# Three reorderings in a two-layer attention and feed-forward kernel: an affine step one fill earlier, a vector step behind the next one, and a weight update behind a small norm

## What is computed

```
x = x + xattn0(ctx, layernorm(x))   # 8 heads of 128; keys and values from [layernorm(ctx)*g+b ; layernorm(x)*g'+b']
x = x + ffn0(layernorm(x))          # GELU(h) with W1 and W2 each plus a small update made from rows of the same batch
x = x + xattn1(layernorm(x), ctx)   # one head of 256
x = x + experts(layernorm(x))       # 8 gated experts, weighted
```

## Time and profile before

| What | Value |
|---|---|
| median of 3 runs (lowest to highest) | 1850.38 us (1848.1 to 1851.29) |
| profiled execution, its own time | 1849.33 us |
| its span in the trace | 1847.5 us, so 1.83 us lie around the span |
| TensorE busy | 1796.0 us, 97% of the span |
| VectorE, ScalarE, GpSimd busy | 79%, 72%, 29% |
| granted TensorE clock, mean | 0.996 of full speed |
| TensorE in the chain of waits that ended last | 80% of the span |

### The profile page before, as it was taken

The page is one execution under the profiler, slowest core; times in us unless marked ns, Lnnn a source line. Parts: engine busy times, 40 slices in busy tenths (PEclk is TensorE's granted clock), DMA queues, the critical chain, the costliest instruction groups (busy, mean ns, idle before and its releaser), DMA issues.

```text
span 1847.5 us, 40072 instructions
## 1 busy us (share of the span) xinstructions
PE 1796.0 (97%) x12874; PEld 1668.1 (90%) x12874; DVE 1464.4 (79%) x3530; ACT 1328.2 (72%) x2554; POOL 535.6 (29%) x700
## 2 busy tenths in 40 slices
PE   7999999999999999999899999999999999999999
PEld 5888888888888888888788999999999999999998
DVE  6888788887888777887667888888888888888876
ACT  4787777877778777777766777677667767766753
POOL 2444334543354433544533111011111111111100
PEclk9999999999999999999999999999999999999999
DMA  4454555645554434444627543333434333343300
GB/s 143 101 137 105 140 131 130 147 97 139 141 129 87 96 79 95 98 85 92 126 67 259 157 89 73 79 66 76 88 59 87 83 68 72 70 87 74 72 7 13
DMA packets 355420, 182.25 MB, mean 99 GB/s; under 512 B 292512, under 2 KB 340512, under 8 KB 355360
## 3 DMA queue, kind: packets, MB, share of 16 engines
q1 hardware_dynamic: 346656, 146.88, 32.9%
q0 software_dynamic: 8704, 34.61, 10.4%
HBM read 97.29 MB, written 21.23 MB: 64 GB/s over the span
## 4 chain that ended last, share of the span: by engine, by line
PE 80%; DVE 9%; issue 4%; ACT 3%; DMA 2%; POOL 1%; SPq 0%; DVEq 0%; POOLq 0%; ACTq 0%
PE ring L2049 9%; PE ring L2051 9%; PE ring L2050 8%; PE ring L741 8%; PE ring L743 8%; PE ring L742 8%; PE sim L2051 3%; PE sim L2049 3%; PE sim L2050 3%; PE sim L741 2%; PE sim L743 2%; PE sim L742 2%; DVE a_parts L664 2%; PE ps_x L741 2%; DVE a_nmax L644 2%
## 5 line engine op out<-in xcount | busy, mean ns | idle before, releaser
L410 POOL TENSOR_SCALAR a_parts<-a_pr,a_rinv 128x512 f16<-128x512 f32 x240 | 173.3, 733 | 489.0 <-DVE a_rinv L655 435.5
L2049 PE MATMUL ring<-b_xch,b_wel 128*128 128x256 f32 x1024 | 289.7, 283 | 0.5 <-DVE b_act_e L1672 0.5
L2051 PE MATMUL ring<-b_xcl,b_weh 128*128 128x256 f32 x1024 | 286.4, 280 | 0.0
L2050 PE MATMUL ring<-b_xch,b_weh 128*128 128x256 f32 x1024 | 286.0, 279 | 0.0
L503 ACT ACTIVATE a_pr<-sim,a_nmax 128x512 f32<-128x512 f32 x256 | 173.1, 683 | 44.2 <-DVE a_nmax L644 43.8
L2050 PEld LDWEIGHTS ring<-b_xch,b_weh 128*128 128x128 f32 x1024 | 193.4, 189 | 0.0
L2049 PEld LDWEIGHTS ring<-b_xch,b_wel 128*128 128x128 f32 x1024 | 192.1, 188 | 0.7 <-DVE b_act_e L1672 0.7
L2051 PEld LDWEIGHTS ring<-b_xcl,b_weh 128*128 128x128 f32 x1024 | 192.1, 188 | 0.0
L644 DVE TENSOR_REDUCE a_nmax<-sim 128x1 f32<-128x512 f32 x256 | 165.0, 681 | 30.3 <-PE sim L743 30.3
L1385 ACT ACTIVATE b_heh<-b_act_e 128x512 fp32r<-128x512 f32 x128 | 80.7, 630 | 146.9 <-DVE b_act_e L1672 113.0
L664 DVE SCALAR_TENSOR_TENSOR a_parts<-a_pr,a_rinv,a_parts 128x512 f16<-128x512 f32 x240 | 178.3, 783 | 0.9 <-POOL a_parts L410 0.9
(11 more groups left out here) (365 smaller groups left out, 6483.6 us busy)
## 6 DMA issues: line engine op xcount, KB each, us to landing
b_w2l_raw<-in_W2T POOLq DMA_DIRECT2D x16, 1088.0 KB, 8.6
b_even_b<-rows_between SPq DMA_DIRECT2D x16, 1024.0 KB, 5.5
b_w1l_raw<-in_W1T POOLq DMA_DIRECT2D x16, 1024.0 KB, 8.3
b_w1l_raw<-in_We SPq DMA_DIRECT2D x8, 768.0 KB, 4.6
expert_halves<-b_w1h SPq DMA_DIRECT2D x8, 768.0 KB, 3.4
expert_halves<-b_w1l SPq DMA_DIRECT2D x8, 768.0 KB, 4.9
b_weh<-expert_halves SPq DMA_DIRECT2D x8, 768.0 KB, 8.7
b_wel<-expert_halves SPq DMA_DIRECT2D x8, 768.0 KB, 10.3
```

What stands on the lines that cost most here:

```text
L410: nc.gpsimd.tensor_scalar(parts[:, 0, t, :], pr[:, h % 2, t, :], rinv[:, h % 2, t:t + 1], 1.0, ALU.mult, ALU.mult).then_inc(prob_ready, 1)
L2049: nc.tensor.matmul(out, ll, rh, start=(n == 0), stop=False)
L2050: nc.tensor.matmul(out, lh, rh, start=False, stop=False)
L2051: last = nc.tensor.matmul(out, lh, rl, start=False, stop=(n == len(parts) - 1))
```

## The change

Three places in the order of ScalarE, VectorE and GpSimd are changed; nothing is added or taken away. First, in every batch but the last, ScalarE does the second affine step (the latents) behind the high half of V7 in slot 4, ahead of that of O3; before it stood behind K7 in slot 5. Second, in batch 0 VectorE takes the maxima of head 1 before the low plane of head 0. Third, GpSimd makes W2's update of batch 0, and issues its DMA, behind `rstd_of(0, "A")`, which belongs to the start of batch 15.

```
@@ ScalarE, the attention's turn
                     if j == 1 and h == H - 4 and nxt:
                         affine(b + 1, 0)
-                    if j == 0 and h == H - 3 and nxt:
+                    if j == 2 and h == H - 4 and nxt:
                         affine(b + 1, 1)
@@ VectorE, ahead of the loop and in the turn
         inverses(0, 0, True)
-        low_parts(0, 0)
 ...
-                if nxt and (prev or h > 0):
+                if nxt:
                     low_parts(b, h)
@@ GpSimd, second stage, ahead(7) and beside(0, "begin")
             if h == 7:
                 rows_rstd(1)
+
+        def beside(h, done):
+            if (h, done) == (0, "begin"):
+                rstd_of(0, "A")
                 update(0, "2", 0)
                 update(0, "2", 1)
                 update(0, "2", 2)
                 update(0, "2", 3)
                 weights_added(0, "2")
-
-        def beside(h, done):
-            if (h, done) == (0, "begin"):
-                rstd_of(0, "A")
```

## The result

| | us |
|---|---|
| changed kernel, median of 4 runs (lowest to highest) | 1832.23 (1831.61 to 1833.32) |
| the kernel before in the same comparison | 1850.23 (1848.1 to 1851.29) |
| ratio, 95% interval | 0.9905 (0.9888 to 0.9922) |
| forecast, range | 1827.7, 1822.5 to 1834 |

The account below looks back on a forecast made before the run. TensorE, busy 97%, was taken as the bound, waiting for the affine step. 18.3 + 1.85 + 3.1 - 0.6 = 22.65 us off 1849.33 gives 1826.7; with 1.05 for the median, 1827.7, range 1822.5 to 1834.

Parts of the forecast that it names:

- Bound and releaser: TensorE, busy 97%, bounds; the affine step, not K7's low half (chance 0.03, 1852.0 us), releases `ps_x` in fifteen batches.
- Edit 1's price: Slot 5, moved affine step: O3's high half 0.25 us late, covered by 1.3 us; batches 1 to 13 gain 18.3 us.
- On TensorE's path this costs nothing.: Slot 5: K7's low half moves from 190.57 to about 190.85, before TensorE needs it at 192.2.
- the 1.41 of the sum: Gain per batch in slot 5: 1.31 us of standing plus 0.10 us for the first product after a wait.
- Batch 0's slot 5: Affine step's move in batch 0: 1.9 us, taken as 1.85 because K7's low half meets TensorE's arrival.
- VectorE takes over: Rival, slot 5 and short slots 1 and 3: a batch keeps only about 1.0 us; 1833.4 us, chance 0.12.
- Edit 2: Batch 0, heads 2 and 3: maxima start 2.7 us earlier, scores of head 3 3.6 us sooner; booked 3.1 us.
- the lower end: Edit 2 gives only 1.0 us if the 1.8 us wait before head 3 brings the lower clock back.
- The seam: Batch 14 into 15: sum +0.6 us of cost, ends +3.0 and -2.5; rival that it keeps its gain: 1824, chance 0.09.
- `b_ln` came early and gave nothing: Seam: `b_ln` starts near 917.2, not 921.30; nothing booked, since any gain ends at W2's landing.
- edit 3 alone: Seam: W2's DMA starts behind W1's landing, 0.1 us cost; rival of 3 us after its update or `b_ln` hold-up: 1830, 0.13.

Follow-up runs that it names:

- Behind the casts: Changed kernel with the latents' affine step one place further down, behind both casts of slot 4, ahead of slot 5's exponentials: 1826.08 us, ratio 0.9874.

## Why the prediction was right in kind and 4.5 us short

- **Bound and releaser: right.** The affine step released `ps_x` and not K7's low half, which the rows named: with the step moved, all fifteen waits went at once, and the projection starts before K7's low half has ended.
- **Edit 1's price: this is the step that failed: "On TensorE's path this costs nothing."** 18.3 us were booked for batches 1 to 13, at 1.41 each; the trace has 12.90, at 0.99. I followed the step's shift into O3's high half and VectorE, and found cover there. I left out the two casts of slot 4, which stand behind O3's high half on ScalarE and feed O4's first product on TensorE. Before, the second ended at 187.70 and O4 began at 187.89: there was hardly any cover to use. In slot 5 a batch gains 1.14 us in the changed kernel. Behind the casts it gains 1.42, as good as the 1.41 of the sum, so that term was right but for the casts. Of the 0.42 us that a batch is short, 0.27 come back there, 3.7 us in all. Batch 0's slot 5 gave 1.48 and not 1.85; behind the casts it gives 1.81.
- **What is left of it, some 0.15 us a batch, lies in slots 0 and 1, and isn't tied to edit 1.** It is no wait. With the step behind the casts, slot 5 gives 1.42 us in every kernel, but slots 0 and 1 together take 0.13 to 0.14 us more than before in four of them and 0.04 in the fifth, which is the one that took 17.9 us off over batches 1 to 13. In the kernels with the step behind V7 it is 0.13 to 0.14 in three and 0.04 to 0.05 in three, and the two kernels without edit 1 lose 0.04 to 0.05 us there too. The products stand a little farther apart: in slot 0 those of 256 columns 0.118 us in the changed kernel and 0.114 in before, whose lists are the same in this slot. What sets this distance is open.
- **VectorE takes over: wrong rival.** Its waits `sim` for `a_ktl` stayed at 9, of 0.3 us each in the steady batches.
- **Edit 2: right in mechanism.** Forecast 3.1, ends 1.0 and 5.2. The waits are 0.82 and 1.57 us (forecast about 1 and 1.8), the distance between the two scores is 6.16 us (33.89 to 40.05; forecast 34.9 to 40.9). In the profiled executions with the edit the lead gained between 19.0 and 66 is 3.2 to 3.3 us in five, 2.9 in one, and 1.7 to 1.8 in five. What parts them is a race that I had not seen. The low half of Wk on VectorE (line 602) stands ahead of the maxima in the chain to head 3's scores, and runs beside GpSimd's high plane (line 410). In the changed kernel, then in the one with W2's high halves later:

```profile
34.63 2.40 POOL L410 TENSOR_SCALAR a_parts<-a_pr,a_rinv 128x512 f16<-128x512 f32 x2 [3.75 <-DMA a_turned<-a_parts]
35.34 1.22 DVE L602 TENSOR_TENSOR a_wkl<-a_wkl_raw,a_wkh 128x1024 fp32r<-128x1024 f32 x1
```

```profile
34.49 1.36 POOL L410 TENSOR_SCALAR a_parts<-a_pr,a_rinv 128x512 f16<-128x512 f32 x2 [3.71 <-DMA a_turned<-a_parts]
35.24 1.67 DVE L602 TENSOR_TENSOR a_wkl<-a_wkl_raw,a_wkh 128x1024 fp32r<-128x1024 f32 x1
```

  In the first, VectorE's step takes 1.22 us and GpSimd's pair 2.40; in the second VectorE's takes 1.67 and the pair 1.36. All eleven executions with the edit fall into these two kinds. The five of the first kind have a second wait of 1.54 to 1.68 us, no low clock behind it, and the gain of 3.2 to 3.3. The six of the second kind have one of 2.08 to 2.14 us; in five of them the clock then fell for 3.4 us, as I had feared for the lower end, and these are the 1.7 to 1.8, while in the sixth it did not fall, which is the 2.9. The same window in the second kernel, at half speed for part of it, and in the first:

```profile
40.00:44.00 4.00, 3.58 (x11) 2.85 (x12) 3.81 (x10) 2.89 (x3) 3.74 (x5) 0.69 0.67 132
```

```profile
40.00:44.00 4.00, 3.74 (x18) 2.88 (x19) 3.81 (x10) 2.66 (x4) 3.82 (x5) 1.00 0.73 137
```

  And the profile of before was itself one of the worse: behind its wait of 3.65 us it had 6.8 us at half speed, while two kernels without edit 2 had 3.4 and gain 0.8 us there. So the edit's mean worth is nearer the 2.4 us measured than 3.3.
- **The seam: -0.9 for -0.6, but the sign is not shown.** It is the sum of batch 14's 0.81, 2.4 lost and 0.7 gained behind. In the second profile of the changed kernel the same sum is -0.15, since 1.5 us are gained behind the seam, where no edit reaches. `b_ln` came early and gave nothing, as said, and it held up nothing either: it ran beside W2's update (899.33 to 900.41), which took 3.73 us against 3.78 before. But two steps of the working were off. W2's DMA didn't start behind W1's landing as forecast: W1 had landed 2.3 us before it (899.1 and 901.41), and the DMA followed its own update by 0.66 us. And I priced edit 3 alone: beside edit 1 it costs 1.4 us at W2's landing. Whether the low clock adds to it is open: beside the seam there are 6.8, 6.8 and 10.2 us of half speed with edits 1 and 3, and 6.8, 3.4 and 3.4 with edit 1 and not 3.
- **Luck in the traced total.** Of the 17.7 us in the trace, 0.90 came before the first scores, and no term of the sum stands for it.

## What to carry to other kernels

When a step is moved up in an in-order list, walk every instruction that it now stands in front of to its reader on the bounding engine, not only the next one, and not only the engine you suspect. Put a step that has 4 us of slack as late as its reader allows, rather than as early as its input does. A high half, a copy or a cast that waits for a landing holds up all that is behind it in its list: look where its own reader is, and move it there; here that alone was worth 4 to 5 us between the traces. And compare the same kernel's traces with each other before a difference of a microsecond is put down to an edit.

## What the runs showed of the hardware

- A second adding DMA of GpSimd never started while the first was in flight: it began 0.26 us behind the first's landing in all seven kernels in which it was ready before, with up to 7.33 us of idle on the engine that issues it. At the seam W2's DMA itself took 11.5 to 12.5 us in thirteen kernels, and 8.7 in the one that made both updates first; why was not tried.
- TensorE's clock at the same place differs from one execution to another of kernels with the same lists there. In batch 0 it stayed at full speed behind waits of 1.54 to 1.68 us in five kernels; behind waits of 2.08 to 2.14 us it fell in five (0.69 over 40 to 44 us in one of them) and stayed in one. At the start of the program, where nothing had been changed, the first products went over from a distance of 0.43 us to 0.23 us at 17.2 us in one execution, 15.7 in another and 18.8 in that of before, which alone gave leads of 0.1 to 1.5 us before the first scores.
- VectorE and GpSimd slow each other in batch 0, and a tenth of a microsecond decides which. Where VectorE's low half of Wk started 0.04 to 0.07 us after GpSimd's second product, it took its usual 1.22 us and the product 1.74 to 1.77 (five executions). Where it started 0.09 to 0.12 us after, it took 1.64 to 1.67 and the product its usual 0.69 (six). Half a microsecond of TensorE's wait hung on it.
